# One block for the projection stage and the windowed attention of the second part, with the first scores and exponentials among the last projection tiles

## The chip, the cores and the metric

The kernel runs on one core of one Trainium2 chip. The metric is the time on the device in microseconds, taken as the median of several runs; lower is better. A core has five engines that run their own instruction queues in order and meet only at semaphores: TensorE (PE, matrix products; PEld are its weight loads), VectorE (DVE), ScalarE (ACT), GpSimd (POOL) and SyncE (SP), which issues DMAs.

## The reference

The program has four parts, each added to a residual stream `x`: a full attention, a windowed attention with a gated MLP, a local attention with latents, and a mixture of experts. The change touches the second part, which has two layers (DEPTH 2) over 2 sequences of 1024 tokens, width 128, 8 heads of 64. Cut to what matters:

```python
def _layer(x, wqkv, qs, ksc, wo, lg, lb, w1, b1, w2, b2):
    h = shift_token(x)
    q, k, v = split(h @ wqkv)                 # 128 -> 3 * 512
    q, k = l2norm(q) * qs, l2norm(k) * ksc
    q, k = rotary_xpos(q, k)
    # windows of 64 queries, each over its own 64 keys and the 64 before
    sim = where(mask, -max, einsum('bhwid,bhwjd->bhwij', 8 * bq, bk))
    o = einsum('bhwij,bhwjd->bhwid', softmax(sim), bv)
    x = x + o @ wo
    h = layernorm(shift_token(x)) * lg + lb
    a, g = split(h @ w1 + b1)
    return x + (a * gelu(g)) @ w2 + b2
```

## The kernel before

Everything stays on the chip, features on partitions: H and XL are 128 x 2048 (width by tokens). A stage is one `nc.Block()`: each engine has a function with its instructions in program order, and at the end of a block all engines meet at a barrier. After the barrier GpSimd clears the semaphores of the stage (`clear`). There is no scheduler: the order on each engine is the order of the code, and the waits are written out (`wait_ge`).

A layer of the second part is, in order: the **projection stage** (block at L1132, semaphores `F1_...`), the **windowed attention** (`window_attention`, L452, semaphores `windows_...`), and a layer norm with the MLP behind it.

The projection stage runs over 16 tiles of 128 tokens (n = 0 to 15), with two sets of buffers (o = n % 2). For one tile:

- TensorE `make(n)` (L1181, L1184): three products of 128 x 512 into banks 2o, 2o+1 (q, k) and bank 4 (v).
- ScalarE `tile(n)`: squares (L1245, semaphore `squared`), copies v (L1246, `v_kept`), stages the input of tile n+2 (L1239), square root of the norms (L1250).
- VectorE `rope(n)`: sum of squares (L1221), rotation (L1223, L1226, L1227, after which `roped` is given and banks 2o, 2o+1 are free), reciprocal (L1229).
- GpSimd `finish(n)`: adds the two halves of the rotation (L1162) and multiplies by the inverse norm (L1165).
- TensorE `turn(n)` (L1192): eight transposes into banks 5 and 6, after both steps of `finish(n)`.
- ScalarE `keep(n)`: copies them to QT (`F_Q`, L1254) and KT (`F_K`, L1255).
- SyncE copies v one half tile further into `F_VS` by DMA (L1148, L1149).

On TensorE the code alternates `make(n)` and `turn(n - 2)`, and ends with `turn(14)`, `turn(15)`; ScalarE ends with `keep(14)`, `keep(15)`.

The windowed attention runs over 16 units n: (sequence, half of it, pair of heads j). Unit 0 and 1 are sequence 0, tokens 0 to 511, head pairs 0 and 1. For one unit:

- TensorE `scores(n)`: the mask (L492, four products) and the scores (L500, sixteen, in the profile 32) into banks 2(n % 2) and the next one. From unit 2 on it waits until exponentials n - 2 are done.
- VectorE `top(n)`: maximum (L555) and its negation (L559).
- ScalarE `exp(n)`: eight exponentials (L609), into one of four buffers: the two halves of XL, then the two halves of `F_raw`, which the projection stage uses as `rs`. Ahead of the first stands the load of the table for exponentials (ACT_TABLE_LOAD).
- VectorE `invert(n)` (L565), GpSimd multiplies (L480), TensorE `turn` (L511), ScalarE and VectorE `keep` (L617, L571), TensorE `mix` (L525), VectorE `put` (L577). At the end TensorE `project` (L533) and VectorE `add` (L581).

`Stage` (L132) is a tuple of the functions of another stage for each engine: `layer_norm` already takes one, to run a following stage inside its own block.

Of the kernel before, what the change touches and what calls it, by code (L numbers as in the profile page):

```python
# [7 lines left out]
P = 128  # L8
# [33 lines left out]
def build(nc, a, out):  # L42
    ctx = ExitStack()
    with ctx, nc.allow_non_contiguous_dma(reason="biases as columns, one element per partition"):
# [52 lines left out]
        with ExitStack() as st:  # L97
            xtok = sb("xtok", [P, NT, P], stack=st)
            with nc.Block() as block:
                @block.sync  # L100
                def _(sp):
                    sp.dma_start(ident[:], a["c_ident"]).then_inc(loaded, 16)
                    sp.dma_start(xtok[:], a["L0_attn_x"].rearrange("b (n p) d -> p (b n) d", p=P)).then_inc(loaded, 16)
# [347 lines left out]

        def window_attention(tag, Q, K, V, VS, masks, prs, pt, scale, weights, dst):  # L452

# [6 lines left out]
            with ExitStack() as st:  # L460
# [11 lines left out]

                with nc.Block() as block:
                    @block.gpsimd
                    def _(pool):
                        for n in range(NG):
                            p = prs[n % NP]
                            pool.wait_ge(inverted, n + 1)
                            pool.wait_ge(exped, n + 1)
                            pool.tensor_tensor(p, p, rs[:, n % 2, :].unsqueeze(2).broadcast_to([P, HW, P]), ALU.mult).then_inc(scaled, 1)  # L480

                    @block.tensor
                    def _(pe):
# [51 lines left out]

                        scores(0)
                        scores(1)
                        for n in range(NG + 1):
# [13 lines left out]
                    def _(dve):  # L552
# [26 lines left out]
                        def add(c):  # L579
                            dve.wait_ge(summed, c + 1)  # L580
                            dve.tensor_tensor(dst[:, cs(c)], dst[:, cs(c)], bank[c], ALU.add).then_inc(added, 1)  # L581

                        top(0)
                        top(1)
# [15 lines left out]
                    @block.scalar  # L600
                    def _(act):
                        def exp(n):
                            act.wait_ge(negated, n + 1)
                            if n >= NP:
                                act.wait_ge(turned, 2 * (n - NP) + 2)
                            if n >= 2:
                                act.wait_ge(inverted, n - 1)
                            for w in range(HW):
                                last = act.activation(prs[n % NP][:, w, :], sview(n)[:, w, :], ACT.Exp, bias=nm[:, n % 2, w:w + 1], scale=scale,  # L609
                                                      accum_out=su[:, n % 2, w:w + 1])  # L610
                            last.then_inc(exped, 1)

                        def keep(n):
                            act.wait_ge(turned, 2 * n + 1)
                            if n >= 2:
                                act.wait_ge(mixed, n - 1)
                            act.activation(pt[:, n % 2, 0:4, :], bank[4].rearrange("p (w n) -> p w n", n=P), ACT.Copy).then_inc(kept_a, 1)  # L617

                        exp(0)
                        for n in range(NG + 1):  # L620
                            if n + 1 < NG:
                                exp(n + 1)
                            if n:
                                keep(n - 1)
                clear(g)

# [490 lines left out]
        with ExitStack() as st:  # L1117
            layer_norm("n3", X, H, add=H, shifted=XL)

            for l in range(LAYERS):  # L1120
                with ExitStack() as sa:
# [9 lines left out]
                                                "turned q_kept k_kept dstep v_moved", st)  # L1131
                    with ExitStack() as sc, nc.Block() as block:  # L1132
                        hs = XL
# [7 lines left out]

                        @block.sync
                        def _(sp, l=l):
                            issue(sp, loaded, hidden_weights(l))
# [7 lines left out]

                        @block.gpsimd
                        def _(pool):
                            for o in range(2):
# [16 lines left out]

                        @block.tensor
                        def _(pe):
                            def make(n, o, first):
# [23 lines left out]
                            with pe.Fori(2, HT) as i:  # L1199
                                for o in range(2):  # L1200
                                    make(2 * i + o, o, False)
                                    turn(2 * i + o - 2, o, False)
                            for o in range(2):
                                turn(NT - 2 + o, o, False)

                        @block.vector
                        def _(dve):
                            def rope(n, o, first):
# [26 lines left out]

                        @block.scalar
                        def _(act):
                            def stage(n, o):
# [28 lines left out]
                            for o in range(2):  # L1267
                                tile(NT - 2 + o, o, False, True)
                                keep(NT - 4 + o)
                            keep(NT - 2)  # L1270
                            keep(NT - 1)
                    clear(g)
                    window_attention("F2", QT, KT, V, VS, mask, [u.rearrange("p (w n) -> p w n", n=P) for u in (XL[:, 0:2 * CH], XL[:, 2 * CH:T])]
                                     + [raw[:, o, :, :].rearrange("p s (w n) -> p (s w) n", n=P) for o in range(2)],
                                     tab[:, :, :, :].rearrange("p o s (w n) -> p o (s w) n", n=P), 8.0,
                                     [F_wo[:, j, :] for j in range(4)], H)

# [986 lines left out]
```

## Time and profile before

| | |
|---|---|
| median of 3 runs | 1331.57 us (1329.58 to 1331.58) |
| profiled execution, time | 1333.07 us |
| profiled execution, span of the core | 1331.3 us, mean granted clock 0.938 |
| PE busy | 1142.0 us (86%) |
| DVE busy | 884.6 us (66%) |
| ACT busy | 592.0 us (44%) |
| POOL busy | 423.8 us (32%) |
| projection stage, layers 1 and 2 | 402.0 to 484.4 us and 613.7 to 696.1 us |
| windowed attention, layers 1 and 2 | 484.6 to 562 us and 696.2 to 773.8 us |

The times in the rows are from the start of the span. A timeline row gives the start, the duration, the engine, the line and the operation, what it writes and reads, the count, and in brackets how long the engine had been idle before and what ended that. A row often holds several instructions in a row on one engine, so its duration is theirs together. The granted clock of TensorE is 1.00 at 2.4 GHz and 0.50 at 1.2 GHz. The two layers of the second part run the same instructions, so most rows shown are of layer 2.

### The profile page before, as it was taken

What the parts mean: (1) busy time and instruction counts of PE and PEld (TensorE: products, weight loads), DVE (VectorE), ACT (ScalarE), POOL (GpSimd) and SP (SyncE); (2) the same over time, 40 slices, a digit from 0 to 9 for tenths busy, and PEclk for the clock granted to TensorE, in tenths of its full rate; (3) what the DMA queues carried; (4) which work ended last, traced back from release to release, by engine and by line L of the source; (5) the groups of instructions that cost most, each with busy time, mean ns of one, the idle gap of its engine ahead of it and who ended that gap; (6) DMA issues with size and microseconds to landing.
All of it is one profiled execution on the core that took longest, in us unless ns stands there. A gap on an engine that the chain in (4) does not pass through costs nothing. (4 is left out here: it accounts for less than half of the span.)

```text
span 1331.3 us, 29020 instructions
## 1 busy us (share of the span) xinstructions
PE 1142.0 (86%) x11396; PEld 689.1 (52%) x11396; DVE 884.6 (66%) x1512; ACT 592.0 (44%) x1392; POOL 423.8 (32%) x374
## 2 busy tenths in 40 slices
PE   7899899899897869998868989576996799984997
PEld 5577645577543448554447754333663354432343
DVE  3777546777457848435967634486566589999687
ACT  2565445665335659334659633301662355520100
POOL 0466301566107955214974420023342000000000
PEclk9899999999999979999988999788996899985999
DMA  3100000200002200011210000000000011100011
GB/s 78 68 7 2 4 9 16 74 1 2 1 1 63 58 18 3 26 42 40 63 36 3 2 1 13 12 4 4 4 5 14 13 20 18 20 9 0 13 30 45
DMA packets 52711, 28.05 MB, mean 21 GB/s; under 512 B 35458, under 2 KB 46188, under 8 KB 52204
## 3 DMA queue, kind: packets, MB, share of 16 engines
q1 hardware_dynamic: 52588, 26.33, 8.0%
q8 instruction: 87, 1.43, 0.4%
q14 instruction: 36, 0.29, 0.1%
HBM read 17.13 MB, written 1.05 MB: 14 GB/s over the span
## 5 line engine op out<-in xcount | busy, mean ns | idle before, releaser
L337 POOL TENSOR_TENSOR A_pr<-A_pr,A_rs 128x1024 f32<-128x1024 f32 x64 | 121.1, 1894 | 66.8 <-DVE A_rs L401 65.6
L391 DVE TENSOR_REDUCE A_mx<-psb 128x1 f32<-128x1024 f32 x64 | 77.8, 1215 | 21.2 <-PE psb L350 21.0
L434 ACT ACTIVATE A_pr<-psb,A_nm 128x1024 f32<-128x1024 f32 x64 | 71.5, 1117 | 22.2 <-DVE A_nm L395 22.0
L1162 POOL TENSOR_TENSOR F_raw<-F_raw,F_rc 128x1024 f32<-128x1024 f32 x32 | 75.6, 2362 | 16.2 <-DVE F_raw L1227 15.6
L361 PE MATMUL psb<-ident,A_pr 128*128 128x128 f32 x512 | 71.6, 284 | 3.1 <-POOL A_pr L337 3.1
L1888 ACT ACTIVATE M_hall<-psb,M_bu 128x512 f32<-128x512 f32 x64 | 44.0, 687 | 61.2 <-PE psb L1830 61.2
L361 PEld LDWEIGHTS psb<-ident,A_pr 128*128 128x128 f32 x512 | 56.2, 144 | 26.0 <-POOL A_pr L337 15.2
L2079 PE MATMUL psb<-M_hb,M_wd 128*128 128x512 f32 x128 | 68.2, 615 | 0.0
L1192 PE MATMUL psb<-ident,F_raw 128*128 128x128 f32 x256 | 37.9, 295 | 34.7 <-POOL F_raw L1165 34.7
L1830 PE MATMUL psb<-XL,M_wu 128*128 128x512 f32 x128 | 65.6, 594 | 0.5 <-ACT M_ST L1897 0.5
L1833 PE MATMUL psb<-XL,M_wg 128*128 128x512 f32 x128 | 65.7, 594 | 0.3 <-DVE M_hall L1937 0.3
L1181 PE MATMUL psb<-F_wqkv,F_hst 128*128 128x512 f32 x128 | 60.6, 595 | 6.1 <-ACT F_hst L1239 4.5
L555 DVE TENSOR_REDUCE F_mx<-psb 128x8 f32<-128x1024 f32 x32 | 39.2, 1224 | 38.7 <-PE psb L500 38.7
L372 PE MATMUL psb<-A_pt,A_V 128*64 128x128 f32 x1024 | 63.0, 276 | 1.7 <-ACT A_pt L441 1.7
L441 ACT ACTIVATE A_pt<-psb 128x512 f32<-128x512 f32 x64 | 38.0, 594 | 55.3 <-PE psb L361 55.3
L824 ACT ACTIVATE G_pt<-psb 128x768 f32<-128x768 f32 x64 | 48.4, 808 | 30.8 <-PE psb L789 30.8
L1165 POOL TENSOR_TENSOR F_raw<-F_raw,F_rn 128x1024 f32<-128x1024 f32 x32 | 60.9, 1902 | 2.5
L1023 POOL TENSOR_TENSOR A_KL<-A_kf,A_KH 128x512 fp32r<-128x512 f32 x16 | 21.0, 1313 | 123.8 <-ACT A_KH L1034 123.8
L1192 PEld LDWEIGHTS psb<-ident,F_raw 128*128 128x128 f32 x256 | 29.7, 149 | 59.2 <-POOL F_raw L1165 59.2
L372 PEld LDWEIGHTS psb<-A_pt,A_V 128*64 128x64 f32 x1024 | 55.3, 137 | 7.1 <-issue 5.0
L2127 DVE TENSOR_TENSOR M_hb<-M_hall,psb 128x512 f32<-128x512 f32 x64 | 43.9, 688 | 20.0 <-PE psb L2089 17.5
L1221 DVE TENSOR_REDUCE psb<-F_sq 128x16 f32<-128x1024 f32 x32 | 39.2, 1224 | 23.2 <-ACT F_sq L1245 22.2
(344 smaller groups left out, 2925.0 us busy)
## 6 DMA issues: line engine op xcount, KB each, us to landing
F_VS<-F_V SPq DMA_DIRECT2D x62, 128.0 KB, 2.3
F_raw<-in_c_xpos_dram SPq DMA_DIRECT2D x3, 1024.0 KB, 4.7
F_wqkv<-in_L_ffn_wqkv_dram SPq DMA_DIRECT2D x3, 768.0 KB, 7.3
A_w<-in_L_attn_w_dram SPq DMA_DIRECT2D x4, 256.0 KB, 3.6
M_wu<-in_L_ffn_Wup_dram SPq DMA_DIRECT2D x16, 64.0 KB, 2.1
M_wg<-in_L_ffn_Wgate_dram SPq DMA_DIRECT2D x16, 64.0 KB, 2.2
M_wd<-in_L_ffn_Wdown_dram SPq DMA_DIRECT2D x16, 64.0 KB, 1.8
M_sel<-in_c_select_dram SPq DMA_DIRECT2D x16, 64.0 KB, 1.9
```

Source lines behind the costliest of these rows:

```text
L337: pool.tensor_tensor(p, p, rs[:, u % 2:u % 2 + 1].broadcast_to([P, SEQ]), ALU.mult).then_inc(scaled, 1)
L361: last = pe.transpose(psb[:, 4 + a2, j * P:(j + 1) * P], pr[:, u % NP, k * P:(k + 1) * P], ident[:])
L372: last = pe.matmul(psb[64 * h:64 * h + 64, 6 + n % 2, 0:P], V[:, (b * TPS + k) * 2 + h, :], pt[:, n % 2, h, k, :], start=(k == 0), stop=(k ...
L391: dve.tensor_reduce(mx[:, u % 2:u % 2 + 1], sview(u), AX, ALU.max).then_inc(maxed, 1)
L434: act.activation(pr[:, u % NP, :], sview(u), ACT.Exp, bias=nm[:, u % 2:u % 2 + 1], scale=scale, accum_out=su[:, u % 2:u % 2 + 1]).then_inc ...
L1162: pool.tensor_tensor(rs[:, o, :], rs[:, o, :], rc[:, o, :], ALU.add).then_inc(unit, 1)
L1165: pool.tensor_tensor(rs[:, o, :].rearrange("p (h d) -> p h d", d=DH), rs[:, o, :].rearrange("p (h d) -> p h d", d=DH), rn[:, o, :].unsquee ...
L1181: pe.matmul(bank[2 * o + i], hst[:, o, :], F_wqkv[:, i * HD:(i + 1) * HD], start=True, stop=True)
L1192: last = pe.transpose(psb[:, 5 + i // 4, (i % 4) * P:(i % 4 + 1) * P], rs[:, o, i * P:(i + 1) * P], ident[:])
L1830: pe.matmul(bank[k], wu[:, b % 3, :], XL[:, cs(c)], start=True, stop=True).then_inc(up_rdy, 1)
L1833: pe.matmul(bank[k + 1], wg[:, b % 3, :], XL[:, cs(c)], start=True, stop=True).then_inc(gate_rdy, 1)
L2079: pe.matmul(bank[4 + c], wd[:, o, :], hb[:, c % 2, :], start=False, stop=True, skip_group_check=True).then_inc(down_n, 1)
```

## The change

`window_attention` gets one more argument, `first`, a `Stage` with the functions of the projection stage. The block of the projection stage is gone: its functions run in the block of the windowed attention, ahead of that stage's own instructions on each engine. So the barrier and the clearing between the two are gone, and both groups of semaphores are cleared at the end. On TensorE `scores(0)` moves ahead of `turn(14)` and `scores(1)` ahead of `turn(15)`, each with a wait that VectorE and ScalarE have read the banks of tiles 14 and 15; ahead of `scores(2)` stand waits for the last copies of q, k and v. On ScalarE `exp(0)` moves ahead of `keep(15)`. VectorE and GpSimd keep their order.

```diff
-        def window_attention(tag, Q, K, V, VS, masks, prs, pt, scale, weights, dst):
+        def window_attention(tag, Q, K, V, VS, masks, prs, pt, scale, weights, dst, first):
...
+                    @block.sync
+                    def _(sp):
+                        first.fetch(sp)
+
                     @block.gpsimd
                     def _(pool):
+                        first.side(pool)
                         for n in range(NG):
...
-                        scores(0)
-                        scores(1)
+                        first.multiply(pe, scores)
...
+                        first.combine(dve)
                         top(0)
                         top(1)
...
-                        exp(0)
+                        first.activate(act, exp)
                         for n in range(NG + 1):
...
-                clear(g)
+                clear(first.flags + g)
...
-                    with ExitStack() as sc, nc.Block() as block:
+                    with ExitStack() as sc:
...
                             for o in range(2):
+                                pe.wait_ge(squared, NT - 1 + o)
+                                pe.wait_ge(roped, NT - 1 + o)
+                                scores(o)
                                 turn(NT - 2 + o, o, False)
...
+                            pe.wait_ge(q_kept, NT)
+                            pe.wait_ge(k_kept, NT)
+                            pe.wait_ge(v_kept, NT)
+                            pe.wait_ge(v_moved, 16 * (2 * NT - 1))
...
                             keep(NT - 2)
+                            exp(0)
                             keep(NT - 1)
-                    clear(g)
```

The queue of TensorE where the projection stage ends, before the change, from `turn(15)` on (L1192 are transposes of a projection tile, L492 and L500 mask and scores of a unit):

```order
L1192 MATMUL psb<-ident,F_raw 128x128 [waits F1_k_kept,F1_q_kept,F1_unit]
L1192 MATMUL psb<-ident,F_raw 128x128 x7
L1132 UNCONDITIONAL_BRANCH
L482 UNCONDITIONAL_BRANCH [waits barrier_Pool_Activation_PE_DVE_SP_release]
L492 MATMUL psb<-F_mask,identb 64x512 x4
L500 MATMUL psb<-F_K,F_Q 64x128 x16
```

The same place with the change, from behind the loop on (L1194 are the transposes, L497 and L505 mask and scores):

```order
L497 MATMUL psb<-F_mask,identb 64x512 [waits F1_roped,F1_squared]
L497 MATMUL psb<-F_mask,identb 64x512 x3
L505 MATMUL psb<-F_K,F_Q 64x128 x16
L1194 MATMUL psb<-ident,F_raw 128x128 [waits F1_k_kept,F1_q_kept,F1_unit]
L1194 MATMUL psb<-ident,F_raw 128x128 x7
L497 MATMUL psb<-F_mask,identb 64x512 [waits F1_roped,F1_squared]
L497 MATMUL psb<-F_mask,identb 64x512 x3
L505 MATMUL psb<-F_K,F_Q 64x128 x16
L1194 MATMUL psb<-ident,F_raw 128x128 [waits F1_k_kept,F1_q_kept,F1_unit]
L1194 MATMUL psb<-ident,F_raw 128x128 x7
L497 MATMUL psb<-F_mask,identb 64x512 [waits F1_v_moved,F1_v_kept,windows_exped,F1_k_kept,F1_q_kept]
```

The scores of unit 0 stand ahead of the transposes of tile 14 and those of unit 1 ahead of tile 15; the barrier is gone, and the scores of unit 2 wait for the last copies of q, k and v beside the exponentials of unit 0.

The queue of ScalarE there before the change, from `keep(15)` on (L1254 and L1255 copy q and k of a tile, L609 are the exponentials of a unit):

```order
L1254 ACTIVATE F_Q<-psb 128x4x128 [waits F1_turned]
L1255 ACTIVATE F_K<-psb 128x4x128
L1132 UNCONDITIONAL_BRANCH
L600 UNCONDITIONAL_BRANCH [waits barrier_Pool_Activation_PE_DVE_SP_release]
L609 ACT_TABLE_LOAD
L609 ACTIVATE XL,F_su<-psb,F_nm 128x128 [waits windows_negated]
L609 ACTIVATE XL,F_su<-psb,F_nm 128x128 x7
```

And with the change, from `keep(14)` on (L1261 and L1262 copy q and k, L614 are the exponentials):

```order
L1261 ACTIVATE F_Q<-psb 128x4x128 [waits F1_turned]
L1262 ACTIVATE F_K<-psb 128x4x128
L614 ACT_TABLE_LOAD
L614 ACTIVATE XL,F_su<-psb,F_nm 128x128 [waits windows_negated]
L614 ACTIVATE XL,F_su<-psb,F_nm 128x128 x7
L1261 ACTIVATE F_Q<-psb 128x4x128 [waits F1_turned]
L1262 ACTIVATE F_K<-psb 128x4x128
```

The table load and the eight exponentials of unit 0 stand between `keep(14)` and `keep(15)`; there is one table load, as before.

## Rows read from the trace of the kernel before

**Rows 1.** Busy us of each engine (instructions) by stretch, with granted clock

```profile
core 0: us, PE busy (x) PEld busy (x) DVE busy (x) ACT busy (x) POOL busy (x), PEclk, DMA share, GB/s
613.70:696.10 82.40, 60.94 (x224) 31.45 (x224) 63.37 (x96) 47.67 (x96) 69.49 (x36) 0.95 0.24 56
696.20:773.80 77.60, 71.16 (x1248) 54.34 (x1248) 47.93 (x84) 54.51 (x273) 30.35 (x16) 0.94 0.01 3
688.00:696.00 8.00, 3.70 (x16) 2.90 (x16) 0.55 (x2) 2.17 (x4) 4.58 (x3) 0.54 0.00 0
709.00:754.00 45.00, 43.95 (x962) 37.14 (x961) 36.91 (x67) 44.31 (x228) 24.94 (x15) 1.00 0.01 3
```

**Rows 2.** Timeline of TensorE, layer 2, around the change of stage

```profile
683.97 1.09 PE L1192 MATMUL psb<-ident,F_raw 128*128 128x128 f32 x8 [0.64 <-POOL F_raw L1165]
688.38 1.74 PE L1192 MATMUL psb<-ident,F_raw 128*128 128x128 f32 x8 [3.31 <-POOL F_raw L1165]
692.86 1.97 PE L1192 MATMUL psb<-ident,F_raw 128*128 128x128 f32 x8 [2.74 <-POOL F_raw L1165]
696.25 0.64 PE L492 MATMUL psb<-F_mask,identb 64*64 64x512 bf16 x4 [1.43 <-PEq L1132]
...
703.09 0.64 PE L492 MATMUL psb<-F_mask,identb 64*64 64x512 bf16 x4 [3.18 <-ACT XL L609]
703.51 1.92 PE L500 MATMUL psb<-F_K,F_Q 64*64 64x128 f32 x32
...
710.18 1.04 PE L500 MATMUL psb<-F_K,F_Q 64*64 64x128 f32 x32
```

**Rows 3.** Timeline of VectorE, layer 2, the same stretch

```profile
688.31 0.24 DVE L1229 RECIPROCAL F_rn<-F_rn 128x16 f32<-128x16 f32 x1
698.66 1.22 DVE L555 TENSOR_REDUCE F_mx<-psb 128x8 f32<-128x1024 f32 x1 [10.11 <-PE psb L500]
...
705.51 1.22 DVE L555 TENSOR_REDUCE F_mx<-psb 128x8 f32<-128x1024 f32 x1 [2.24 <-PE psb L500]
706.77 0.17 DVE L559 TENSOR_SCALAR F_nm<-F_mx 128x8 f32<-128x8 f32 x1
```

**Rows 4.** Timeline of ScalarE, layer 2, the same stretch

```profile
684.29 0.59 ACT L1246 ACTIVATE F_V<-psb 128x512 f32<-128x512 f32 x1
...
690.64 0.59 ACT L1255 ACTIVATE F_K<-psb 128x512 f32<-128x512 f32 x1
694.86 0.60 ACT L1254 ACTIVATE F_Q<-psb 128x512 f32<-128x512 f32 x1 [3.62 <-PE psb L1192]
695.35 0.59 ACT L1255 ACTIVATE F_K<-psb 128x512 f32<-128x512 f32 x1
696.22 1.28 ACT L609 ACT_TABLE_LOAD   x1 [0.27 <-PEq L1132]
700.13 0.37 ACT L609 ACTIVATE XL<-psb,F_nm 128x128 f32<-128x128 f32 x1 [2.63 <-DVE F_nm L559]
...
702.88 0.41 ACT L609 ACTIVATE XL<-psb,F_nm 128x128 f32<-128x128 f32 x1
...
706.98 0.37 ACT L609 ACTIVATE F_raw<-psb,F_nm 128x128 f32<-128x128 f32 x1 [1.14 <-DVE F_nm L559]
```

**Rows 5.** DMA issues of the page: KB each, median us from issue to landing

```profile
F_VS<-F_V SPq DMA_DIRECT2D x62, 128.0 KB, 2.3
```

**Rows 6.** Timeline of ScalarE, end of another stage: a table load with nothing waited for

```profile
785.82 1.28 ACT L1338 ACT_TABLE_LOAD   x1
787.11 0.20 ACT L1338 ACTIVATE warm<-eps 128x1 f32<-128x1 f32 x1
```

**Rows 7.** Timeline of all engines, layer 1, the same places

```profile
478.82 0.59 ACT L1255 ACTIVATE F_K<-psb 128x512 f32<-128x512 f32 x1
...
491.46 0.64 PE L492 MATMUL psb<-F_mask,identb 64*64 64x512 bf16 x4 [3.19 <-ACT XL L609]
...
495.35 0.37 ACT L609 ACTIVATE F_raw<-psb,F_nm 128x128 f32<-128x128 f32 x1 [1.14 <-DVE F_nm L559]
```

## What I predict

> **What bounds the kernel now.** I read the stages by stretch first. In the projection stage the busiest engine is GpSimd, 69.49 of 82.40 us; in the windowed attention from 709 to 754 us two engines are full: ScalarE 44.31 of 45.00 and TensorE 43.95, at a granted clock of 1.00 [rows 1]. ScalarE's missing 0.69 us lie at the very end of that stretch. So from unit 2 on this stage is a train that ScalarE pulls without a gap, and what comes before the train is what can be won: whatever brings the first exponential of unit 2, at 706.98 [rows 4], forward brings the whole rest forward by as much.
>
> Then I read the change of stage engine by engine. TensorE does the transposes of tiles 13, 14 and 15 at 683.97, 688.38 and 692.86, and is idle for 3.31 and 2.74 us before the last two, waiting for GpSimd [rows 2]. VectorE has nothing to do from 688.55 to 698.66, 10.11 us [rows 3]. ScalarE waits 3.62 us before `keep(15)`, then through the barrier, and its table load at 696.22 is followed by the first exponential only at 700.13, which VectorE's maximum released [rows 4]. From 688 to 696 us the engines are busy for 3.70 (PE), 0.55 (DVE), 2.17 (ACT) and 4.58 us (POOL) of 8.00 [rows 1]: a fill and a drain one after the other. The chain of the fill is scores(0), maximum, exp(0), exp(1) beside scores(2), maximum(2), exp(2).
>
> **The change part by part, layer 2.**
>
> *scores(0) ahead of turn(14).* Its wait is for tile 14 in banks 0 and 1; the transposes of tile 13 end at 685.06 and the rotation of tile 14 is over by then (the one of tile 15 ends at 688.3, a tile earlier is some 4.4 us less). It takes 0.42 + 1.92 = 2.4 us at the lower clock (703.09, 703.51 and the end at 705.43) or about 1.3 at the higher (1.04 for the 32 at 710.18) [rows 2]. Either way it is done by 687.5, ahead of 688.38, when turn(14) may start. Cost nothing; the cover is TensorE's idle 3.31 us.
>
> *scores(1) ahead of turn(15).* It starts when turn(14) ends, 690.12, and takes up to 2.4: 692.5. turn(15) is released by GpSimd at 692.86. Cost nothing, with 0.3 us to spare; without that cover it would push keep(15) only past exp(0), see below, so even 0.5 us more is hidden.
>
> *top(0) on VectorE.* VectorE is free at 688.31 + 0.24 = 688.55. Maximum and negation take 705.51 to 706.98, 1.47 us [rows 3, 4], so the release of exp(0) is at 690.0.
>
> *exp(0) ahead of keep(15) on ScalarE.* keep(14) ends at 690.64 + 0.59 = 691.23. Then the table load. Where nothing is waited for, the next instruction follows the load's start after 787.11 - 785.82 = 1.29 us [rows 6]. So exp(0) starts at 692.54 and not at 700.13. A unit's eight exponentials take 702.88 - 700.13 = 2.75 us [rows 4]: 695.29. Behind it is queued keep(15), whose input is there at 694.83 [rows 2]; it is held up by 0.43 us and its copy of k ends 695.35 + 0.59 - 694.86 = 1.08 us after its start: 696.37. exp(1) begins at 696.3 (702.88 before), its maximum is there at 692.5 + 1.47 = 694.0.
>
> *The waits before scores(2).* q and k: 696.37. v: its last copy ends at 684.88 [rows 4], the DMA of it takes 2.3 us [rows 5], so 688. exp(0): 695.4. So scores(2) starts at 696.40, before at 703.09 [rows 2]: 6.69 us earlier. GpSimd, VectorE and the PSUM banks behind it are idle there.
>
> *From there on.* scores(2) to exp(2) took 706.98 - 703.09 = 3.89 us. I keep that, since TensorE will again have been mostly idle just before and be at 1.2 GHz as in [rows 2]. exp(2) then starts at 700.29; exp(1) ends at 699.05, so ScalarE waits as before. Shift 6.69 us.
>
> *Barrier and clearing.* keep(15) ended at 695.94 and the table load began at 696.22 [rows 4], so 0.28 us, already within the 6.69. One more group of semaphores is cleared at the end, where 0.2 us separate the stages: zero.
>
> **Layer 1** by the same steps: keep(14) ends at 478.82 + 0.59 = 479.41; + 0.02 + 1.29 + 2.75 = 483.47; + 1.08 + 0.03 = 484.58 for scores(2), before 491.46: 6.88 us; exp(2) at 488.47 and not 495.35 [rows 7].
>
> **Sum:** 6.69 + 6.88 = 13.6 us. The profiled execution took 1333.07 us (span 1331.3), so 1319.5 for it; it lay 1.5 us above the median of 1331.57, from which 13.6 off is 1318.0.
>
> *A rule against it.* The rows show 1.29 us from a table load to the next instruction. The Trainium skill, "ScalarE: Activation LUTs", section "What ACT_TABLE_LOAD costs", gives some 1283 ns for the load and 1380 ns more for a drain, 2.66 us for each switch of table. In the kernel before such a drain would have been hidden in the wait at 700.13; now it would stand on the path in both layers. By the rule as an estimate the gain would be 2 x 1.38 = 2.8 us less. The load of [rows 6] has no such gap behind it, so I go by the row.
>
> **The rivals.**
>
> *A. As worked out:* 1318.0. Chance 0.60.
>
> *B. TensorE stays at 2.4 GHz.* scores(0) fills the idle time after which the clock fell: transposes took 1.09 us at 683.97, 1.74 and 1.97 later, and the mean clock from 688 to 696 is 0.54 [rows 1, 2]. If it stays up through turn(14), keep(14) comes 1.74 - 1.09 = 0.65 us earlier in each layer: 1316.7. If it were up in scores(2) too, 1.92 - 1.04 = 0.88 more in each: 1314.9. Against it: the scores fill only about a third of the gap, and before scores(2) TensorE does nothing but turn(15) for 3.9 us. The Trainium skill, "TensorE: Matmul & The Clock Gate", section "Part 1: The HAM clock gate (the "warmup" mystery)", says "the default state is throttled, and activity releases the throttle", which is on B's side for turn(14) and on A's for scores(2). Chance 0.20.
>
> *C. A dead time on ScalarE behind the table load,* seen as a gap between load and first exponential with the maximum long there. A second load's length in each layer, 2 x 1.28: 1320.6. For it speaks that the load of this place was never seen without a wait behind it; against it [rows 6]. It is the skill's rule above as a mechanism. Chance 0.08.
>
> *D. Half of it:* one layer's fill is caught by something that I don't see, say a late `roped` or DMA of v: 1325. Chance 0.05.
>
> *E. No gain:* the stage behind waits for something that this stage does not set, a load say. Its DMA share is 0.01 [rows 1], so nothing is in flight to be waited for. 1331.6. Chance 0.03.
>
> *F. Slower: exp(0) blocks keep(15).* ScalarE's queue is in order, and keep(15) is now behind a wait for VectorE, which is behind TensorE's wait for `roped` of tile 14. If exp(0) were released only where it was, at 700.13, keep(15) would come behind it and exp(1) and scores(2) 0.98 us later than before (two copies), so +2.0 us: 1333.5. It decides where exp(0) starts later than 692.54 + 6.7 = 699.2; the maximum would have to come 9 us after VectorE is free. Chance 0.04.
>
> **How the numbers follow.** The predicted time is A's, 1318.0. Everything behind moves forward by 7 and then by 14 us, and the stretches of lower clock elsewhere fall differently; eight transposes cost 0.88 us more at the lower clock [rows 2], so a few such give 1 to 2 us either way. The runs of before spread over 2 us. The range is 1314.5 to 1321.0: A with 1.5 to 3 us on either side, nearly all of B and most of C; D, E and F are left out (0.12), and some of the tails of the others. A measurement can tell about 0.2%, 2.7 us, from no change: A to D are beyond it, faster 0.93; same 0.03; slower 0.04 (F's 2 us would be at that edge, and I count it there).
>
> **What would show it right or wrong.** In the new profile: mask and scores of unit 0 between the transposes of tiles 13 and 14, and turn(14) and turn(15) still released by GpSimd; the maximum directly behind the last reciprocal of the projection, not 10 us later; the table load 0.02 us behind keep(14) and the first exponential 1.29 us behind its start; copies of q and k of tile 15 straight after the eighth exponential; scores(2) released by that copy; from exp(2) on a ScalarE without gaps and the 45 us stretch unchanged. The step most likely wrong is the clock between turn(14) and scores(2), and with it which of scores(2) or exp(1) sets exp(2). A wait of TensorE on turn(15) by scores(1), or a maximum that comes late, would make the prediction wrong by whole microseconds.

## The result, and the profile after

| | before | with the change |
|---|---|---|
| median | 1331.57 us (1329.58 to 1337.38, 4 runs) | 1317.69 us (1317.38 to 1318.82, 4 runs) |
| ratio | | 0.9886 (95% interval 0.9861 to 0.9911) |
| span of the profiled execution | 1331.3 us | 1315.6 us |
| mean granted clock | 0.938 | 0.945 |

The change takes 13.9 us off the median; 13.6 were forecast, 1318.0 us. The interval of the ratio puts it between 11.9 and 18.5 us.

First TensorE in layer 2, which answers to [rows 2]. L1194 are the transposes of tiles 13, 14 and 15, L497 and L505 mask and scores:

```profile
672.57 1.09 PE L1194 MATMUL psb<-ident,F_raw 128*128 128x128 f32 x8 [0.63 <-POOL F_raw L1168]
673.59 0.41 PE L497 MATMUL psb<-F_mask,identb 64*64 64x512 bf16 x4
673.83 1.04 PE L505 MATMUL psb<-F_K,F_Q 64*64 64x128 f32 x32
677.10 1.09 PE L1194 MATMUL psb<-ident,F_raw 128*128 128x128 f32 x8 [2.23 <-POOL F_raw L1168]
678.12 0.41 PE L497 MATMUL psb<-F_mask,identb 64*64 64x512 bf16 x4
678.37 1.04 PE L505 MATMUL psb<-F_K,F_Q 64*64 64x128 f32 x32
681.47 1.09 PE L1194 MATMUL psb<-ident,F_raw 128*128 128x128 f32 x8 [2.06 <-POOL F_raw L1168]
684.60 0.64 PE L497 MATMUL psb<-F_mask,identb 64*64 64x512 bf16 x4 [2.04 <-ACT F_K L1262]
685.00 1.95 PE L505 MATMUL psb<-F_K,F_Q 64*64 64x128 f32 x32
```

The scores of units 0 and 1 lie in idle time: turn(14) and turn(15) still wait for GpSimd, now 2.23 and 2.06 us where it was 3.31 and 2.74. scores(2) is released by the copy of k of tile 15, as the working had it. What differs from the working is the clock: both tiles' transposes take 1.09 us and not 1.74 and 1.97, and TensorE is at its lower level again only for scores(2), after 2.04 us of idleness. In layer 1 the order and the releasers are the same, but turn(15) starts after 1.18 us of idleness and takes 1.97 us, at the lower level.

ScalarE, answering to [rows 4] (L1261 and L1262 are the copies of q and k of tiles 14 and 15; of L614 the first exponentials of units 0, 1 and 2 are shown):

```profile
678.23 0.60 ACT L1261 ACTIVATE F_Q<-psb 128x512 f32<-128x512 f32 x1 [2.44 <-PE psb L1194]
678.73 0.59 ACT L1262 ACTIVATE F_K<-psb 128x512 f32<-128x512 f32 x1
679.33 1.28 ACT L614 ACT_TABLE_LOAD   x1
680.63 0.37 ACT L614 ACTIVATE XL<-psb,F_nm 128x128 f32<-128x128 f32 x1
...
683.38 0.63 ACT L1261 ACTIVATE F_Q<-psb 128x512 f32<-128x512 f32 x1
683.86 0.64 ACT L1262 ACTIVATE F_K<-psb 128x512 f32<-128x512 f32 x1
684.34 0.42 ACT L614 ACTIVATE XL<-psb,F_nm 128x128 f32<-128x128 f32 x1
...
688.48 0.37 ACT L614 ACTIVATE F_raw<-psb,F_nm 128x128 f32<-128x128 f32 x1 [1.18 <-DVE F_nm L563]
```

From 678.23 to the first exponential of unit 2 ScalarE has one gap, the 1.18 us right before it; before, it stood still for 3.62 and 2.63 us and at the barrier. The first exponential comes 1.30 us after the table load's start.

By stretch, the fill and the train behind it, answering to the last two of [rows 1]:

```profile
core 0: us, PE busy (x) PEld busy (x) DVE busy (x) ACT busy (x) POOL busy (x), PEclk, DMA share, GB/s
676.50:684.50 8.00, 3.40 (x52) 2.68 (x52) 5.06 (x7) 6.24 (x22) 5.46 (x4) 0.91 0.00 0
690.50:735.50 45.00, 43.59 (x960) 36.77 (x958) 36.78 (x67) 44.29 (x228) 24.95 (x15) 1.00 0.02 4
```

The 8 us after the last reciprocal of the projection now hold 6.24 us of ScalarE and 5.06 of VectorE, where there were 2.17 and 0.55. The 45 us behind the first exponential of unit 2 are what they were.

**A measure that other stages can't blur.** The two profiled executions already differ before the changed code begins. The table load of the norm that closes the first part of the program, ahead of the projection stage of layer 1, stands at 388.16 before and at 382.57 after:

```profile
388.16 1.28 ACT L213 ACT_TABLE_LOAD   x1 [2.97 <-PEq L146]
```

```profile
382.57 1.28 ACT L213 ACT_TABLE_LOAD   x1 [2.97 <-PEq L146]
```

That is 5.6 us in code that the change doesn't touch. It isn't the other program around it either: in a second profile of the very same changed kernel (told below, under "What is left on the path") this load stands at 386.61, 4.0 us later than in the first. So I measure in each trace from R, the start of the last reciprocal of the projection stage (688.31 in [rows 3]), to the table load of the norm behind the windowed attention (774.00 before, 755.49 after in layer 2). The figures below are in us from R, and all are starts except the ends of the transposes:

| kernel, layer | turn(14) ends | turn(15) ends | exp(0) | scores(2) | exp(2) | next norm |
|---|---|---|---|---|---|---|
| before, 1 | 1.60 | 6.51 | 11.81 | 14.77 | 18.66 | 85.68 |
| before, 2 | 1.81 | 6.52 | 11.82 | 14.78 | 18.67 | 85.69 |
| change, 1 | 1.27 | 6.53 | 3.71 | 7.75 | 11.62 | 78.64 |
| change, 2 | 1.28 | 5.65 | 3.71 | 7.69 | 11.56 | 78.57 |

The change gives 7.04 and 7.12 us, 14.2 together. From exp(2) to the next norm it is 67.0 us in all four rows: here every us at exp(2) reaches the next stage (two layers of the experiments, told below, are exceptions). The spans differ by 15.7; 14.2 are the change's and 1.5 are what the unchanged parts happened to differ by in these two executions.

### The profile page after: what moved, and what is told of

Read it like the earlier page. It is cut to its first block and busy times, and to the rows that moved or that the text cites. A ratio compares the mean times of both kernels' runs of the same rounds, so it can differ in the third digit from the quotient of the medians.

```text
span 1315.6 us, 29004 instructions
## 1 busy us (share of the span) xinstructions
PE 1135.4 (86%) x11396; PEld 684.0 (52%) x11396; DVE 886.7 (67%) x1512; ACT 591.1 (45%) x1392; POOL 423.8 (32%) x374
## 5 line engine op out<-in xcount | busy, mean ns | idle before, releaser
L1194 PE MATMUL psb<-ident,F_raw 128*128 128x128 f32 x256 | 35.9, 284 | 28.1 <-POOL F_raw L1168 28.1
L1194 PEld LDWEIGHTS psb<-ident,F_raw 128*128 128x128 f32 x256 | 28.2, 144 | 53.0 <-POOL F_raw L1168 53.0
```

The lines of the kernel that those rows point to most:

```text
L1194: last = pe.transpose(psb[:, 5 + i // 4, (i % 4) * P:(i % 4 + 1) * P], rs[:, o, i * P:(i + 1) * P], ident[:])
```

## The experiments

The theory was that the gain is the fill of the second stage (scores, maximum, table load, exponentials), taken out of the path by laying it into the drain of the first. The rivals: it is the barrier; it is TensorE's clock; or only one of the moves matters. The first four kernels below ran beside a median of before of 1333.4 us (22 runs). All edits are shown against the changed kernel, and a ratio is always to the kernel before, from the runs beside it.

**One block only.** The moves undone, the block kept:

```diff
                             for o in range(2):
+                                turn(NT - 2 + o, o, False)
+                            for o in range(2):
                                 pe.wait_ge(squared, NT - 1 + o)
                                 pe.wait_ge(roped, NT - 1 + o)
                                 scores(o)
-                                turn(NT - 2 + o, o, False)
...
                             keep(NT - 2)
-                            exp(0)
                             keep(NT - 1)
+                            exp(0)
```

> One block, but scores(0) and scores(1) behind turn(15) and exp(0) behind keep(15): the change without its moves. If the gain is the fill of the second stage taken off the path, little is left: scores(0) starts where turn(15) ends and no longer behind the last copies and the barrier, 1.4 us earlier in each layer, so some 2.8 us off before's 1331.6: 1328.8. If the barrier and the clearing between the stages were what cost, it gives most of the change's 13.9 us: 1318 to 1320.

Measured: 1328.88 us (1325.78 to 1337.62, 10 runs), ratio 0.9974 (0.9946 to 1.0002). From R, the next norm comes at 84.12 in layer 1 and 84.99 in layer 2: 1.56 and 0.70 us off, not 7 (the ratio alone would leave room for no gain at all). The barrier was not what cost. In layer 1 exp(2) was at 17.10, 1.56 us earlier than before. In layer 2 it was at 15.99, 2.7 us earlier, because scores(2) ran at the higher clock there (0.41 + 1.07 us and not 0.64 + 1.95); but 2.0 of it were given back inside the train:

```profile
696.00:700.00 4.00, 2.58 (x64) 2.15 (x59) 1.50 (x3) 3.83 (x23) 3.10 (x2) 0.69 0.02 4
700.00:704.00 4.00, 4.00 (x48) 3.15 (x44) 2.19 (x4) 3.59 (x20) 1.00 (x2) 0.50 0.00 0
704.00:708.00 4.00, 4.00 (x96) 3.35 (x92) 2.79 (x5) 2.77 (x16) 1.70 (x2) 0.96 0.02 4
```

These are stretches of that kernel, columns as above. From 700 to 704 us, at a granted clock of 0.50, TensorE is busy all the time and falls behind. ScalarE, which pulls the train at 1.00, then waits twice for transposes of a unit (L516), the second time when the clock has just come back, and is down to 2.77 of 4.00 us in the last row:

```profile
701.76 0.60 ACT L622 ACTIVATE F_tab<-psb 128x512 f32<-128x512 f32 x1 [0.41 <-PE psb L516]
706.38 0.60 ACT L622 ACTIVATE F_tab<-psb 128x512 f32<-128x512 f32 x1 [1.23 <-PE psb L516]
```

These two waits are 1.6 of the 2.0 us. TensorE is a near second in this stage, and an earlier start isn't worth its whole length where the train meets the low clock.

**Scores early, exponentials late.** Only the move on ScalarE undone:

```diff
                             keep(NT - 2)
-                            exp(0)
                             keep(NT - 1)
+                            exp(0)
```

> As the change, but exp(0) behind keep(15). If the fill's chain counts, table load and exponentials wait for the last copy: exp(0) at 1.3 us behind its end, scores(2) 2.75 us later, so 2.9 us earlier than before in each layer and not 7: 1325.8. If TensorE's clock, kept up by the early scores, were the source, the scores stand where they do in the change and the time is 1318 to 1319.

Measured: 1327.63 us (1325.54 to 1333.89, 10 runs), ratio 0.9955 (0.9931 to 0.9979). From R: exp(0) 8.08, exp(2) 15.01, the next norm 82.02 and 82.03: 3.66 us off in each layer. The chain said 2.9; the 0.8 more is turn(15), which ran at the higher clock in both layers and ended at 5.64 and not 6.5. The theory of the clock alone, 1318 to 1319, is out: TensorE's queue is that of the change, and half of the gain is gone. So of the 7.1 us of a layer the place of exp(0) is worth 3.4.

**scores(1) late.** The scores of unit 1 behind turn(15), all else as in the change:

```diff
-                            for o in range(2):
-                                pe.wait_ge(squared, NT - 1 + o)
-                                pe.wait_ge(roped, NT - 1 + o)
-                                scores(o)
-                                turn(NT - 2 + o, o, False)
+                            pe.wait_ge(squared, NT - 1)
+                            pe.wait_ge(roped, NT - 1)
+                            scores(0)
+                            turn(NT - 2, 0, False)
+                            turn(NT - 1, 1, False)
+                            pe.wait_ge(squared, NT)
+                            pe.wait_ge(roped, NT)
+                            scores(1)
```

> As the change, but scores(1) behind turn(15). By the chain: scores(1) and scores(2) follow each other on TensorE, 2.4 us each at the lower clock, then 1.47 us for the maximum, so exp(2) is 0.8 to 1.5 us later than in the change in each layer: 1319.5 to 1321. If only exp(0) matters and the rest is covered: 1317.7.

Measured: 1323.2 us (1321.48 to 1324.34, 7 runs), ratio 0.992 (0.9891 to 0.9949), which of 1331.57 is 1320.9. From R: exp(2) 12.89 and 12.47, the next norm 79.94 and 79.53, so 1.3 and 1.0 us later than the change. The chain holds, though not by the link I named. VectorE and ScalarE in layer 2:

```profile
690.03 1.22 DVE L559 TENSOR_REDUCE F_mx<-psb 128x8 f32<-128x1024 f32 x1 [5.72 <-PE psb L505]
```

```profile
691.49 0.37 ACT L614 ACTIVATE XL<-psb,F_nm 128x128 f32<-128x128 f32 x1 [1.98 <-DVE F_nm L563]
```

It is exp(1) that waits for its maximum, 1.98 us, and exp(2) follows exp(1) without a gap.

**The clock, kept up by products that nobody reads.** First with many: 8 ahead of turn(15) and 12 behind it, into a bank that is free there.

```diff
+                                if o:
+                                    for i in range(8):
+                                        pe.matmul(psb[:, 7, 0:P], centre[:], ident[:], start=True, stop=True)
                                 turn(NT - 2 + o, o, False)
+                            for i in range(12):
+                                pe.matmul(psb[:, 7, 0:P], centre[:], ident[:], start=True, stop=True)
```

> As the change, with products that nobody reads in TensorE's idle time: 8 before turn(15), 12 between turn(15) and scores(2) in each layer. If the clock is what is left in the fill, scores(2) takes 1.3 and not 2.4 us and exp(2) comes up to 1.1 us earlier in each layer: 1315.5 to 1316.5. If exp(1) or the copies set exp(2), or the products themselves hold scores(2) up, it is 1317.7 or more.

Measured: 1321.14 us (1316.38 to 1321.94, 4 runs), ratio 0.9886 (0.9832 to 0.9941). TensorE in layer 2, the products being L1211 and L1214:

```profile
681.05 1.93 PE L505 MATMUL psb<-F_K,F_Q 64*64 64x128 f32 x32
682.91 2.74 PE L1211 MATMUL psb<-ident,centre 128*128 128x128 f32 x16
685.48 1.04 PE L1194 MATMUL psb<-ident,F_raw 128*128 128x128 f32 x8
686.36 2.84 PE L1214 MATMUL psb<-ident,centre 128*128 128x128 f32 x24
689.13 0.41 PE L497 MATMUL psb<-F_mask,identb 64*64 64x512 bf16 x4
```

The clock is up for turn(15) and scores(2), but the products are no longer in idle time: turn(15) starts 5.72 us behind R, where GpSimd would have let it go at 4.56, and scores(2) at 9.37, where it was 7.69. From R: exp(2) 12.37 and 12.19, the next norm 80.84 and 79.20, so 2.2 and 0.6 us later than in the change. In layer 1 1.4 us of that were lost behind exp(2), where TensorE stood still for 2.12 us, came back at the lower clock, and ScalarE waited 1.22 us for its transposes. There were too many products, as the second case of the expectation had it, so this kernel said nothing on what the clock is worth. Repeated with 4 and 4:

> As the change, with only 4 products that nobody reads ahead of turn(15) and 4 behind it in each layer, few enough for TensorE's idle time (2.0 us before turn(15), 1.0 to 1.9 us before scores(2)). If the clock is what keeps exp(2) back and they hold it up, turn(15) takes 1.1 us, scores(2) 1.3 and exp(2) starts 10.5 us behind the last reciprocal of the projection stage and not 11.6: 1315.6. If the clock falls anyway, or only turn(15) profits, 11.5 and 1317.7.

Measured: 1317.73 us (1314.29 to 1323.64, 8 runs) beside a median of before of 1330.05; ratio 0.9904 (0.9879 to 0.9929). From R: exp(2) 10.49 and 10.31, the next norm 77.51 and 77.33, so 1.1 and 1.2 us off the change, as the first theory said. turn(15) took 1.06 and 1.04 us and the products of scores(2) 1.07; scores(2) itself started no earlier than in the change (7.68 and 7.50). The whole time doesn't show it: its runs spread over 9 us. I take the stretch as the measurement of the mechanism and leave open whether this kernel's median is lower than the change's.

**What is left on the path.** Three edits of the change, and the change again, side by side (before 1332.06).

> The change itself once more, beside the next three, which are edits of it. From the last reciprocal of the projection stage to the table load of the next norm it had 78.6 us in each layer (before 85.7). Expected again: 78.6, and 1317 to 1319.

Measured: 1317.96 us (1317.06 to 1322.75, 4 runs), ratio 0.9903 (0.987 to 0.9937). From R to the next norm 79.00 and 78.64. In its layer 1 turn(14) ended at 1.68, the lower clock, and exp(0) came at 4.12, scores(2) at 8.10 and exp(2) at 11.98.

The table load early:

```diff
+                            act.activation(warm[:], eps[:, 0:1], ACT.Exp)
                             keep(NT - 2)
                             exp(0)
                             keep(NT - 1)
```

> As the change, with the table of exponentials loaded in ScalarE's idle time ahead of keep(14). exp(0) then starts 1.1 us earlier, 2.6 us behind the last reciprocal and not 3.7, when the negated maximum is there. If the table load is on the path, exp(2) comes 1.1 to 1.3 us earlier in each layer and the time is 1315.3. If keep(15), which waits for the transposes of tile 15, sets exp(1) and scores(2) as soon as exp(0) is earlier, no more than 0 to 0.8 us in each: 1316.5 to 1317.7.

Measured: 1318.14 us (1316.69 to 1319.2, 4 runs), ratio 0.9892 (0.9864 to 0.9919): no gain that the times show. From R: exp(0) 2.68 and 2.59, as expected; exp(2) 10.51 and 10.75, the next norm 77.52 and 77.76, so 1.1 and 0.8 us less than the change (1.5 less than layer 1 of its second profile, where the two transposes ran at the same clocks as here), more than the second case allowed in layer 1. keep(15) now waits for turn(15), by 0.19 us in layer 2.

exp(1) ahead of keep(15), and the waits for the last copies in a function that is called behind scores(3), ahead of the first transposes of the attention:

```diff
                             exp(0)
+                            exp(1)
                             keep(NT - 1)
...
                                 scores(n + 2)
+                            if n == 1:
+                                settle()
...
-                            if n + 1 < NG:
+                            if 0 < n < NG - 1:
                                 exp(n + 1)
...
-                            pe.wait_ge(q_kept, NT)
-                            pe.wait_ge(k_kept, NT)
-                            pe.wait_ge(v_kept, NT)
-                            pe.wait_ge(v_moved, 16 * (2 * NT - 1))
+                            def settle():
+                                pe.wait_ge(q_kept, NT)
+                                pe.wait_ge(k_kept, NT)
+                                pe.wait_ge(v_kept, NT)
+                                pe.wait_ge(v_moved, 16 * (2 * NT - 1))
+                            return settle
```

> As the change, with exp(1) ahead of keep(15) too, and the waits for the last copies behind scores(3), ahead of the first transposes that need their banks. If keep(15) is the link between exp(0) and scores(2), scores(2) starts 6.6 us behind the last reciprocal and not 7.7, and exp(2) 1.0 us earlier in each layer: 1315.6. If TensorE (turn(15) at the lower clock, then scores(2)) holds it, 0: 1317.7.

Measured: 1315.73 us (1314.74 to 1318.9, 4 runs), ratio 0.9885 (0.9856 to 0.9914). From R: scores(2) 6.67 and 6.47, exp(2) 10.34 and 10.16, the next norm 77.36 and 77.18. keep(15) was the link between exp(0) and scores(2): 1.0 us expected, 1.3 to 1.4 measured against the 78.6 of the change. Some 0.2 of it is that scores(2) took 1.70 and not 1.95 us, the clock coming back within it. TensorE is no longer idle before scores(2): it follows turn(15), which ended at 6.53 in both layers.

Both:

> Both of the two before this: scores(2) is then set by the end of turn(15), 5.7 to 6.5 us behind the last reciprocal. exp(2) 1.2 to 2.0 us earlier than in the change in each layer: 1313.7 to 1315.3. If the early table load is hidden anyway, it is not faster than with exp(1) moved alone: 1315.6.

Measured: 1314.27 us (1314.01 to 1315.19, 4 runs), ratio 0.9868 (0.9842 to 0.9895). From R: turn(15) ends 5.64 and 6.53, scores(2) 5.64 and 6.45, exp(2) 9.16 and 10.05, the next norm 76.27 and 77.07. Now TensorE's turn(15) sets scores(2), and what sets exp(2) depends on its clock. In layer 2, with turn(15) at the lower clock, TensorE's chain is the later one: exp(2) waits 0.79 us for its maximum. In layer 1, with turn(15) and scores(2) at the higher clock, the negated maximum is there at 8.43, and exp(2) follows keep(15) on a ScalarE that has had no gap since exp(0): there ScalarE's own queue sets it, and the layers differ by 0.9 us at exp(2) where the maxima are 1.6 us apart. So a few products ahead of turn(15) should pay only where the clock is low:

> As the best version so far (table load early, exp(1) ahead of keep(15)), with 4 such products ahead of turn(15). There turn(15) and scores(2) follow each other at once and set exp(2), at 9.2 us behind the last reciprocal where turn(15) ran at the higher clock and 10.1 where it ran at the lower. If the products hold the clock up: 9.2 in both layers, 1313.5. If not, as without them: 1314.3.

Measured: 1311.18 us (1310.37 to 1311.72, 4 runs) beside 1330.05; ratio 0.9854 (0.9816 to 0.9893). From R: exp(2) 9.05 and 9.04, the next norm 76.18 in both layers. TensorE in layer 2, the products being L1213:

```profile
678.22 1.92 PE L505 MATMUL psb<-F_K,F_Q 64*64 64x128 f32 x32
680.07 1.45 PE L1213 MATMUL psb<-ident,centre 128*128 128x128 f32 x8
681.36 1.04 PE L1196 MATMUL psb<-ident,F_raw 128*128 128x128 f32 x8
682.32 0.41 PE L497 MATMUL psb<-F_mask,identb 64*64 64x512 bf16 x4
682.56 1.04 PE L505 MATMUL psb<-F_K,F_Q 64*64 64x128 f32 x32
```

This is the best version: it beats both kernels, the change by 2.4 us in each layer from R on. The ratios of this kernel and the one before it overlap in their intervals; what sets it ahead is the stretch, down by 0.1 and 0.9 us. In both layers exp(2) now follows keep(15) without a gap, so ScalarE is full from exp(0) on, and exp(0) is what is left: it waits for the negation of its maximum, which ends at 2.56. No run combined this kernel with the next edit.

**The negation that took 1.20 us.** In the profile of the change VectorE's negation of the maxima (L563) was slow twice, beside GpSimd's work on tile 15:

```profile
677.08 2.36 POOL L1165 TENSOR_TENSOR F_raw<-F_raw,F_rc 128x1024 f32<-128x1024 f32 x1
678.27 1.20 DVE L563 TENSOR_SCALAR F_nm<-F_mx 128x8 f32<-128x8 f32 x1
679.51 1.90 POOL L1168 TENSOR_TENSOR F_raw<-F_raw,F_rn 128x1024 f32<-128x1024 f32 x1
680.74 0.70 DVE L563 TENSOR_SCALAR F_nm<-F_mx 128x8 f32<-128x8 f32 x1
```

It ends at 679.47 and 681.44, and GpSimd's operations at 679.44 and 681.41. The test writes the maxima of units 0 and 1 to PSUM:

```diff
-                            dve.tensor_reduce(mx[:, n % 2, :], sview(n), AX, ALU.max).then_inc(maxed, 1)
+                            m = mx[:, n % 2, :] if n >= 2 else psb[:, 7, 64 + HW * n:64 + HW * (n + 1)]
+                            dve.tensor_reduce(m, sview(n), AX, ALU.max).then_inc(maxed, 1)
...
-                            dve.tensor_scalar(nm[:, n % 2, :], mx[:, n % 2, :], -scale, None, ALU.mult).then_inc(negated, 1)
+                            dve.tensor_scalar(nm[:, n % 2, :], m, -scale, None, ALU.mult).then_inc(negated, 1)
```

> As the change, but the maxima of units 0 and 1 are written to PSUM and negated from there. In the change the negation of unit 0 took 1.20 us, and 0.17 before. If it waits for GpSimd's multiply of tile 15 because both work on SBUF, it takes 0.2 us now, with no effect on the time (1317.7), as exp(0) waits for the table load. If it was slow for another reason, such as the first run of that code, it stays at 1.20.

```profile
678.51 2.37 POOL L1166 TENSOR_TENSOR F_raw<-F_raw,F_rc 128x1024 f32<-128x1024 f32 x1
679.71 0.17 DVE L564 TENSOR_SCALAR F_nm<-psb 128x8 f32<-128x8 f32 x1
```

0.17 us in the middle of GpSimd's operation, for unit 0 in both layers and for unit 1 in layer 2 (in layer 1 unit 1 meets no GpSimd operation and took 0.17 already in the change); exp(0) is at 3.68 and 3.73 from R and the next norm at 78.64 and 78.60, unmoved. One run gave 1315.16 us, which alone says nothing.

The trace of before had shown it all along. In the middle of its train, 11 times in each layer, a negation starts shortly before GpSimd's multiplication ends, takes 0.29 us and not 0.17, and ends 0.02 or 0.03 us behind it (706.77 in [rows 3] meets none). The first of layer 2:

```profile
714.24 1.90 POOL L480 TENSOR_TENSOR F_raw<-F_raw,F_rs 128x1024 f32<-128x1024 f32 x1 [1.72 <-DVE F_rs L565]
715.88 0.29 DVE L559 TENSOR_SCALAR F_nm<-F_mx 128x8 f32<-128x8 f32 x1
```

## Why the prediction was right

**The path.** Right: the start of exp(2) was all that counted. It moved by 7.04 and 7.11 us and the next norm by 7.04 and 7.12.

**scores(0), scores(1), top(0).** Right that they cost nothing; turn(14) and turn(15) still wait for GpSimd, 2.21 and 1.18 us in layer 1, 2.23 and 2.06 in layer 2. But top(0) takes longer than I wrote: 1.47 us for maximum and negation, measured 679.47 - 677.08 = 2.39. I took the 1.47 from unit 2, whose negation meets no GpSimd operation, and here it runs beside the two steps of tile 15. It was still hidden, by 1.2 us, behind the table load: luck, as the working never looked at this. In layer 2 of the kernel with an early table load, and in both layers of the best version, it is the very thing that sets exp(0).

**Table load.** 1.29 us taken, 1.29 and 1.30 measured. The 1.38 us of drain that go with each load by the Trainium skill, "ScalarE: Activation LUTs", section "What ACT_TABLE_LOAD costs", are not borne out by this trace: the next instruction starts 1.29 and 1.30 us after the load's start, and the load itself right behind the copy before it. Rival C is out.

**exp(0) ahead of keep(15), and scores(2).** Right: layer 1 of the change's second profile, where turn(14) ran at the lower clock, has exp(0) at 4.12, scores(2) at 8.10 and exp(2) at 11.98 from R; the working gives 692.54 - 688.31 = 4.23, 8.09 and 11.98.

**The clock: this is the term that was mis-sized.** The forecast took A, the clock down before turn(14)'s end. In both layers of the profiled execution it was rival B's first half: turn(14) took 1.09 us, exp(0) came at 3.71, and a layer gained 7.0 or 7.1 and not 6.9 or 6.7. The second half of B, scores(2) at 2.4 GHz, did not come: it took 0.64 + 1.95. So the working's sum of 13.6 should have been 14.2. B's own price was too high: it took the 0.65 us by which the transposes are shorter, but the faster turn(14) also starts later (0.19 from R, where the slow ones of before and of the second profile started between -0.04 and 0.07), so in layer 2 its end came 0.53 us earlier than before, and scores(2) came at 7.69 where the working had 8.09. In the other profile of the change layer 1 was A and layer 2 B, so which of the two one sees changes from run to run. I had given B a third of A's chance, and it came in 3 of these 4 layers. Over all 11 profiles that have the early scores(0), and with it the same order on TensorE up to turn(14), this turn(14) took 1.09 us in 15 of 22 layers, 1.31 to 1.44 in 3 and 1.69 or 1.70 in 4: B's first half is the usual course.

**The medians.** 13.9 us is nearer to 13.6 than the mechanism deserves: that is luck, as unchanged code moves by several us between executions and the interval alone is 6.6 us wide. The range of 1314.5 to 1321.0 was drawn for this and held.

**D, E, F.** Nothing of them: both layers gave the same, nothing behind waited, and exp(0) held keep(15) back by only 0.8 us where turn(15) ran at the higher clock (5.65 to 6.46 from R in layer 2), and not at all where it ran at the lower.

## What to carry to other kernels

Where one stage drains while the next one fills, look for what the fill needs (here tiles 0 to 3 and a free pair of banks, not the last tile) and put its chain, table load included, into the drain; without the barrier but with the order kept a layer gained 1.56 or 0.70 us, and the moves brought that to 7.0 or 7.1. Then ask link by link what sets the first unit of the steady train, since each link removed (exp(0), scores(1), keep(15), the table load, the clock) only helps until the next one is late. Measure such edits from a fixed event to the next stage in the trace; whole times carry the noise of all the rest.

## What the runs showed that I had not expected

**VectorE's negation of 8 numbers a partition waits out a GpSimd operation.** 1.20 and 0.70 us in SBUF, ending 0.03 us behind GpSimd's end, and 0.17 with the input in PSUM. It shows in the train of before as well, as 0.29 us. The Trainium skill, "SBUF — State Buffer", section "Who interferes with whom", has a rule for it: a `tensor_scalar` can enter a two-port mode of VectorE, whose second pair of ports is shared with GpSimd; whoever issues first has the pair for the whole instruction, and the other "fully blocks". The traces agree in when the negation ends; that it ran in such a mode no trace shows. 8 numbers a partition were enough to be blocked.

**A few unread products are worth something, more are not.** In the three kernels that have them turn(15) took 1.04 to 1.06 us and the products of scores(2) 1.04 to 1.07 in all six layers; in the two profiles of the change turn(15) took 1.97 in two of four layers and scores(2) 1.95 in all four. 4 ahead of turn(15) and 4 behind it were worth 1.1 and 1.2 us a layer against the change; 4 ahead of it alone 0.1 and 0.9 against the version with both edits. With 8 and 12 turn(15) started 1.3 and 1.2 us late, and the next norm came 2.2 and 0.6 us later than in the change.

**Unchanged code moves.** By 388 us into the span, in code that is the same in all of them, the 13 profiles stand up to 5.6 us apart, and the two of the changed kernel 4.0, while a stage measured from R repeats to 0.1 us when TensorE's clock takes the same course.
